# Cross-attention in fp32: the sum of the probabilities over six chunks as three additions in place of one strided reduction

## The reference, cut to what matters

```
q = emb @ Wq + bq                        # emb: (16, 100, 512)
k = latent @ Wk + bk                     # latent: (16, 722, 256)
v = latent @ Wv + bv
w = softmax((q @ k^T) * scale, axis=1)   # over the 100 tokens
pred = w @ v
x = pred + emb
out = (x - mean(x)) * rsqrt(var(x) + 1e-6) * gamma + beta
```

## Time and profile before

| what | value |
|---|---|
| median of three runs | 144.66 us (144.46 to 144.82) |
| the profiled execution, its own time | 144.95 us |
| its span, from the first to the last instruction | 143.2 us |
| around the span | 1.75 us |
| PE busy | 134.4 us (94%) |
| DVE busy | 117.3 us (82%) |
| ACT busy | 81.6 us (57%) |
| POOL busy | 65.2 us (46%) |
| the 16 chunk sums (L690) | 19.8 us of DVE, 1239 ns each |

### The profile page before, as it was taken

One profiled execution on the slowest core, in us unless ns is written; L12 is line 12 of the kernel. 1 busy time (PEld: TensorE's weight loads), 2 busy tenths in 40 slices (PEclk: granted clock), 3 DMA queues, 4 the chain that ended last, 5 costly groups with the idle time before them and its releaser, 6 DMA issues.

```text
span 143.2 us, 2969 instructions
## 1 busy us (share of the span) xinstructions
PE 134.4 (94%) x1046; PEld 129.4 (90%) x1046; DVE 117.3 (82%) x216; ACT 81.6 (57%) x286; POOL 65.2 (46%) x61
## 2 busy tenths in 40 slices
PE   6998999999899999999999999999999999999910
PEld 6998999999898999999999999999999999998900
DVE  0689989999777899759999975899699976876992
ACT  4677349459527836385564729475665628483520
POOL 1000000009031594735758472666667463659891
PEclk9999999999999999999999999999999999999996
DMA  4999999965057597897896889699897886545113
GB/s 141 300 406 421 421 300 395 317 213 194 5 205 237 195 307 243 328 346 259 314 311 259 322 256 402 215 316 326 252 306 250 331 273 225 217 146 178 73 73 146
DMA packets 10670, 37.33 MB, mean 261 GB/s; under 512 B 1184, under 2 KB 1184, under 8 KB 10656
## 3 DMA queue, kind: packets, MB, share of 16 engines
q1 hardware_dynamic: 9424, 34.92, 69.5%
q10 hardware_dynamic: 1232, 2.23, 4.1%
HBM read 33.87 MB, written 3.28 MB: 259 GB/s over the span
## 4 chain that ended last, share of the span: by engine, by line
PE 75%; DVE 10%; DMA 4%; POOL 3%; issue 2%; ACT 2%; SPq 1%; POOLq 1%
PE ps_U L400 28%; PE ps_S L386 27%; PE ps_Y L421 12%; DMA xT_in<-xT 4%; DVE xT_lo L647 3%; PE ps_U L361 3%; DVE xu L659 2%; PE ps_Y L361 2%; POOL xT_in L848 2%; PE ps_w L409 1%; SPq L255 1%; DVE wkq L637 1%; DVE W_lo L744 1%; POOL xT_in L836 1%; POOL rstd L841 1%
## 5 line engine op out<-in xcount | busy, mean ns | idle before, releaser
L521 ACT ACTIVATE expo<-scores,negmax 121x100 f32<-121x100 f32 x96 | 35.0, 366 | 27.3 <-DVE negmax L679 27.3
L386 PE MATMUL ps_S<-G,ctxT_in 128*121 128x100 f32 (+1 forms) x384 | 43.5, 270 | 0.0
L400 PEld LDWEIGHTS ps_U<-prob,ctx_in 121*128 121x128 f32 x360 | 42.1, 192 | 0.9
L400 PE MATMUL ps_U<-prob,ctx_in 121*128 121x100 f32 x360 | 42.5, 274 | 0.0
L386 PEld LDWEIGHTS ps_S<-G,ctxT_in 128*121 128x121 f32 (+1 forms) x384 | 42.0, 185 | 0.0
L825 POOL TENSOR_TENSOR prob<-expo,rinv 121x600 f32<-121x600 f32 x16 | 19.0, 1189 | 35.7 <-DVE rinv L686 35.7
L841 POOL TENSOR_TENSOR rstd<-vareps,neg_half 128x1 f32<-128x1 f32 (+1 forms) x13 | 12.4, 955 | 22.8 <-DVE vareps L717 22.5
L836 POOL TENSOR_TENSOR xT_in<-x_in,xT_in 128x512 f32<-128x512 f32 (+1 forms) x13 | 16.6, 1276 | 13.0 <-issue 8.4
L690 DVE TENSOR_REDUCE probsum<-prob 121x100 f32<-121x600 f32 x16 | 19.8, 1239 | 3.0 <-POOL prob L825 2.7
L521 ACT ACTIVATION_READ_ACCUMULATOR expo<-scores,negmax 121x1 f32 x96 | 18.0, 187 | 0.0
L675 DVE TENSOR_TENSOR scores<-ps_S,c_rows 121x600 f32<-121x600 f32 x16 | 12.5, 782 | 5.8 <-PE ps_S L386 5.6
(11 more groups left out here) (91 smaller groups left out, 175.8 us busy)
## 6 DMA issues: line engine op xcount, KB each, us to landing
ctx_in<-ctx SPq DMA_DIRECT2D x16, 768.0 KB, 5.7
ctxT_in<-ctxT SPq DMA_DIRECT2D x16, 722.0 KB, 5.2
xT_in<-xT SPq DMA_DIRECT2D x8, 400.0 KB, 8.8
x_in<-x SPq DMA_DIRECT2D x12, 256.0 KB, 4.7
out<-xT_in ACTq DMA_DIRECT2D x8, 256.0 KB, 4.2
wqk<-Wqk SPq DMA_DIRECT2D x4, 388.0 KB, 4.3
out<-xT_in SPq DMA_DIRECT2D x3, 256.0 KB, 2.0
wv_in<-Wv SPq DMA_DIRECT2D x1, 512.0 KB, 16.1
```

The costliest lines, as they stand in the source:

```text
L386: last = nc.tensor.matmul(ps_scores(c)[0:rows(c), :], ctxT_in[:, q, l * M + c * MP:l * M + c * MP + rows(c)], G[:, l, bass.ds(b * T, T)], ...
L400: last = nc.tensor.matmul(ps_U[:, q, l * T:(l + 1) * T], ctx_in[0:rows(c), q, c, l * P:(l + 1) * P], prob[0:rows(c), q, c * T:(c + 1) * T] ...
L521: last = nc.scalar.activation(expo[0:MP, q, c * T:(c + 1) * T], scores[0:MP, q, c * T:(c + 1) * T], ACT.Exp, bias=negmax[0:MP, q, c:c + 1] ...
```

## The change

`chunk_sum` becomes three dependent additions on DVE. The first adds chunks 3 to 5 to chunks 0 to 2, 300 numbers for each partition, into a new buffer `probhalf`. The second adds the first two hundreds of `probhalf` into `probsum`. The third adds the last hundred. Each range is contiguous. Both inputs of each addition lie in SBUF, where the reduction had one input. Two semaphores are new, `probhalf_set` and `probpair_set`. POOL may write `prob` again after the first addition (`probhalf_set`) where it waited for the whole sum before.

```
+        probhalf = sb("probhalf", [P, 2, HALF * T])
...
+        probhalf_set = sem("probhalf_set")
+        probpair_set = sem("probpair_set")
...
             def chunk_sum(b, q):
                 dve.wait_ge(prob_set, b + 1)
-                nc.vector.tensor_reduce(probsum[0:MP, batch_tokens(b)], prob[0:MP, q, :].rearrange("p (c t) -> p t c", t=T),
-                                        AX.X, ALU.add).then_inc(probsum_set, 1)
+                nc.vector.tensor_tensor(probhalf[0:MP, q, :], prob[0:MP, q, 0:HALF * T], prob[0:MP, q, HALF * T:MC * T],
+                                        ALU.add).then_inc(probhalf_set, 1)
+                dve.wait_ge(probhalf_set, b + 1)
+                nc.vector.tensor_tensor(probsum[0:MP, batch_tokens(b)], probhalf[0:MP, q, 0:T], probhalf[0:MP, q, T:2 * T],
+                                        ALU.add).then_inc(probpair_set, 1)
+                dve.wait_ge(probpair_set, b + 1)
+                nc.vector.tensor_tensor(probsum[0:MP, batch_tokens(b)], probsum[0:MP, batch_tokens(b)],
+                                        probhalf[0:MP, q, 2 * T:3 * T], ALU.add).then_inc(probsum_set, 1)
...
                 if not first_two(b):
                     pool.wait_ge(U_done, b - 1)
-                    pool.wait_ge(probsum_set, b - 1)
+                    pool.wait_ge(probhalf_set, b - 1)
```

## The result

The changed kernel took 147.82 us in the median of six runs (147.53 to 148.54), the kernel before 144.75 us in six runs beside it (144.46 to 145.14). The ratio is 1.0218, with a 95% interval from 1.0191 to 1.0245: 2.2% slower, some 3.1 us. The forecast was 147.3 us, 1.8% slower. The upper end of the range, 147.9, is where the measured time lies: the median is just inside, and the ratio times 144.75, 147.91 us, just outside.

The account below looks back on a forecast made before the run. PE bounds the kernel from 36.26 to 132.22 us, waiting for DVE only at the two ends. Head 0.96 plus tail 1.70 us on the 144.66 us median gave 147.3 us, 1.8% slower; range 145.9 to 147.9 us.

Parts of the forecast that it names:

- What the additions cost by themselves: Each sum on DVE, nothing beside it: 0.47, 0.26, 0.26 and 0.06 between, 1.05 us in all, 0.19 less than now.
- rival (a): Tail, batch 15: the second addition gets in ahead of POOL, only the third is held; 146.1 us in all, chance 0.18.
- That they are held by POOL: DVE additions with two SBUF inputs wait for a POOL instruction issued first; the one-input reduction can't be held.
- Rival (d): Head and tail: POOL doesn't hold the additions at all; tail 0.35 us earlier, 144.3 us in all, chance 0.07.
- The price of a held instruction: A held addition ends its own streaming time behind POOL's end: 0.31 us for 300 numbers, 0.10 for 100.
- The head: Batch 0: POOL's L864 holds the first addition, so PE gets xu_lo 0.96 us later, with bounds 0 and 1.2.
- The tail: Batch 15: POOL's two instructions hold the second and third additions; sum and end 1.70 us late, bounds -0.35 and +2.2.
- The 0.1 us of delay: Tail, batch 15: added to POOL's L848, queued behind L836, putting its end at 133.29 us.
- The middle: The 14 sums between head and tail: each saves 0.19 us on DVE, worth nothing because PE is the bound.
- Rival (c): Tail hardly moves, because POOL yields between its instructions; the head's 0.96 us alone, 145.6 us in all, chance 0.06.
- the frame of the sum: Whole execution: 0.96 + 1.70 = 2.66 us put on the profiled 144.95 us, giving 147.61, and on the median 144.66.
- The chance of 0.60: Chance given to the forecast's own course: first addition held in the head, second and third in the tail, 147.3 us.

Follow-up runs that it names:

- e3: The changed kernel with batches 0 and 15 summed by the one strided reduction again, the 14 between by three additions; ratio to the kernel before 0.9981.
- e1: The changed kernel with batch 0 summed by the one strided reduction again, batches 1 to 15 by three additions; ratio to the kernel before 1.0136.
- e2: The changed kernel with batch 15 summed by the one strided reduction again, batches 0 to 14 by three additions; ratio to the kernel before 1.0063.
- e4: The kernel before with only batches 0 and 15 summed by three additions, the other 14 by the reduction; ratio to the kernel before 1.0187.
- e5: The changed kernel with POOL's long head instruction (lower half of Wv) moved behind batch 1's probabilities, PE waiting at first use; ratio to the kernel before 1.0104.
- e7: As e5, but batch 15 summed by the one strided reduction, batches 0 to 14 by additions; ratio to the kernel before 0.9960.
- e11: As e5, with one more wait: POOL starts the residual of tile 11 only after batch 15's sum; ratio to the kernel before 1.0002.
- e8: The kernel before with each sum made by two dependent one-input reductions, 600 numbers to 300 and 300 to 100; ratio to the kernel before 1.0005.
- e9: The kernel before with 32 more DVE instructions, tiny memsets of scratch columns, four in each of turns 4 to 11; ratio to the kernel before 1.0024.
- e10: The kernel before with 64 more DVE instructions, tiny memsets of scratch columns, eight in each of turns 4 to 11; ratio to the kernel before 0.9987.

## Why the prediction was right in kind and too small

**What the additions cost by themselves.** 0.47, 0.26, 0.26 and 0.03 between, as forecast. The rule of 58 cycles plus one a number (the Trainium skill, VectorE: DVE Perf Modes, section on the TRN2 errata), by which rival (a) got its chance, gives 0.37 and 0.16; the 14 free sums of e3 took 0.47 and 0.26 in the median, and refute it. The same section says of this row that it comes out too low, and gives (N + 151)/0.96 ns for an fp32 tensor_tensor of N numbers. That is 0.47 and 0.26 us, and the trace agrees; the prediction left this formula out.

**That they are held by POOL.** Shown. The additions were long only beside a POOL instruction (the change, e1, e2, e4, the tail of e5, the sum of batch 1 in e5 and e7), and of their own length when it was moved (e5) or made to wait (e11). Reductions in the same place weren't held (e8). Rival (d) falls. The price of a held instruction, POOL's end plus its own streaming time, was right: 0.32 and 0.33 measured for 300 numbers (0.31 forecast), 0.11 to 0.14 for 100 (0.10). The other held instructions of the 14 traces fit in: 6 numbers ended 0.01 to 0.03 us behind POOL, 400 numbers 0.42 to 0.44, 512 numbers 0.54 to 0.56.

The Trainium skill, SBUF — State Buffer, section "Who interferes with whom", says that a DVE instruction with two SBUF inputs and a GpSimd instruction that reads SBUF shut each other out for the whole of the one that issued first, and that a reduction never contends. The traces agree for a DVE instruction that comes second, and for the reduction. They don't for POOL's rstd, which has two SBUF inputs and held nothing. That POOL waits for DVE in its turn shows only faintly: where POOL began 0.21 to 0.23 us before the end of such a DVE instruction it took 1.35 to 1.37 us (e2, e4, e5), where 0.04, it took 1.30 (the change).

One reading of the prediction goes with this: it has the last L721 held by the pair of L848 and by L841, POOL's rstd. L721 ended at 139.56, 0.54 behind the pair's end at 139.02 and 0.40 before the end of L841, so that it was held by the pair alone.

**The head.** Forecast 0.96 us. The heads with additions took 6.21, 6.38 and 6.39 us, those with the reductions and the long POOL instruction in its place 5.26 to 5.42: in the mean 6.33 against 5.34, 0.99 us. The heads fall in two groups: POOL's long instruction began 2.30 to 2.32 us behind PE's second pair in the change, e1, e3 and e9, and 2.47 or 2.48 us behind it in before, e2, e4, e8 and e10. Like with like the additions cost 6.21 - 5.26 = 0.95 us and 6.39 - 5.41 = 0.98 us, which is the forecast. The profiles of before and of the change are of different groups, and so differ by 0.81 us only. What puts an execution into one group or the other isn't known.

**The tail.** Forecast 1.70 us, measured 12.49 - 10.82 = 1.67. The order of events is that of the forecast, step by step. POOL's L845 began 0.04 us before the first addition was done and 0.08 before the second was issued, and by this small margin it was not rival (a); the first margin was 0.04 us in e1 too, and 0.05 in e5. The 0.1 us of delay that the forecast gave POOL's second instruction didn't come. The weight sum came 1.17 us later behind that of tile 11 (4.21 against 3.04), where 1.3 was forecast.

**The middle.** No cost and no gain: 92.86 against 92.92 us. Rival (c), in which POOL yields between its instructions, was wrong in the tail: a held addition did get through between two of POOL's, but the next one was too late.

**The step that failed is the frame of the sum.** Its two terms came as forecast (0.99 + 1.67 = 2.66 us). But the forecast put 0.96 + 1.70 on the profiled execution's own 144.95 us and by that took the 1.75 us around the span as a constant: a term of its own, put at nothing without a reason. It grew by 0.37. With it, 144.95 + 2.66 + 0.37 = 147.98 us, against 147.72 measured for the profiled execution; of the difference 0.15 us lies in the head (0.81 for 0.96, the two groups above), 0.06 in the middle and 0.03 in the tail. And 144.66 + 3.03 = 147.7 us stands against the median of 147.82. e9 shows the same 0.35 us without any addition. What makes the time around the span grow, no run shows. The bounds of the range were drawn from the head and the tail alone, with no room for this.

**The chance of 0.60** for the forecast's own chain of events was low, looking back: the margin in the tail was small, but it came out the same each time. In all four profiles in which the additions stand in the tail without the extra wait (the change, e1, e4 and e5) the tail took 12.48 to 12.53 us.

## What to carry to other kernels

Before one DVE instruction is replaced by several, compare their inputs too: a reduction has one, an addition two, and a DVE instruction with both inputs in SBUF stood still beside each POOL instruction that began first, rstd excepted. One with an input in PSUM didn't. Busy time doesn't show whether that matters; list each place where the instruction stands, and see what POOL runs there and who waits for DVE. Here 14 of 16 places were free and worth nothing, and the other two cost 2.6 to 2.7 us. The same reading pays the other way round: moving one POOL instruction away from a DVE instruction that PE waits for made the kernel before 0.5% faster. And a sum that is put on a whole execution takes the time around the span as fixed, which it wasn't here; the range has to leave room for it.

## What the runs showed that I had not expected

- **The time around the span goes with DVE's number of instructions** in these kernels, and not steadily: 1.74, 1.95, 2.1 and again 1.72 us with at most 28, 30, 32 and 64 more instructions than before. Whether the number itself does it or something that goes with it, none of these runs shows. A difference of 0.2% between two kernels can be this alone.
- **Reductions with a stride don't all cost the same.** 600 numbers in sixes, 100 apart, took 1.24 us, while the same 600 in pairs, 300 apart, took 0.79 us, and 300 in threes, 100 apart, 0.50. The groups of e8:

```profile
L700 DVE TENSOR_REDUCE probhalf<-prob 121x300 f32<-121x600 f32 x16 | 12.7, 792 | 3.5 <-POOL prob L850 3.1
L703 DVE TENSOR_REDUCE probsum<-probhalf 121x100 f32<-121x300 f32 x16 | 8.0, 499 | 0.5
```

  At 1.04 ns a number and 159 of base the two would be 0.78 and 0.47, so that only the one in sixes is slow, and a stride of 100 or 300 by itself doesn't do it. Whether it is the six, the 600 that one result spans or something else wasn't tried.
- **Moving POOL's instruction in the head gave more than PE's idle time**: 0.57 us by start times for 0.41 us of idle time. PE's first product behind a wait took 0.42 us, the same product without a wait 0.35 (e5: 35.90 us). Where the rest of the difference comes from isn't known.
